# First two products with w1 of the first chunk, computed in halves of 256 rows

## The reference

```
x = x + tanh(g_xattn) * cross_attention(layernorm(x), ctx)     # 16 heads of 32, 154 keys a batch
h   = relu(layernorm(x) @ w1.T + b1)                           # 2048 hidden features
hq  = float_quantize(h, 4, 3)                                  # 8-bit float
out = float_quantize(hq @ float_quantize(w2, 4, 3).T + bq, 5, 10)
x = x + tanh(g_ffn) * out
```

## Time and profile before

| | us |
|---|---|
| median of 3 runs | 1613.96 (1610.55 to 1615.25) |
| the profiled execution | 1612.67 |
| its span, first to last instruction | 1610.9 |
| PE busy in the span | 1533.0 (95%) |
| PE idle in front of `hidden(0, 0)` | 7.2 |
| mean granted TensorE clock, share of full speed | 0.987 |

### The profile page before, as it was taken

How to read it: one execution, slowest core, us unless ns; L and a number is a source line. 1 busy time by engine, 2 the same in 40 slices (tenths; PEclk the granted TensorE clock), 3 DMA queues, 4 the chain that set the end, 5 groups by cost and what they waited for, 6 DMA issues and landing times.

```text
span 1610.9 us, 23580 instructions
## 1 busy us (share of the span) xinstructions
PE 1533.0 (95%) x8576; PEld 694.5 (43%) x8576; DVE 944.7 (59%) x1297; ACT 813.1 (50%) x1196; POOL 877.4 (54%) x919
## 2 busy tenths in 40 slices
PE   7875999999999999999999999999999999999998
PEld 4421444444444444444444444444444444444443
DVE  7787465675756566564656656465665656446231
ACT  4665664635545463555546455554645455454411
POOL 3788464554736455474646547464654746445320
PEclk9997999999999999999999999999999999999999
DMA  8356463544544454344435444344543434333120
GB/s 335 94 156 147 135 144 103 140 105 115 112 132 100 113 135 103 105 114 137 103 110 135 113 99 110 125 101 125 136 114 102 110 120 102 99 99 85 43 53 26
DMA packets 252856, 186.70 MB, mean 116 GB/s; under 512 B 160013, under 2 KB 209477, under 8 KB 251077
## 3 DMA queue, kind: packets, MB, share of 16 engines
q1 hardware_dynamic: 252740, 185.19, 42.9%
HBM read 99.95 MB, written 51.59 MB: 94 GB/s over the span
## 4 chain that ended last, share of the span: by engine, by line
PE 72%; DVE 13%; POOL 5%; issue 5%; DMA 1%; ACT 1%; SPq 1%; DVEq 0%; ACTq 0%
PE ring L514 52%; PE ring L708 8%; PE m_ps L616 4%; DVE y L1014 3%; PE s_ps L646 2%; DVE bns L1039 2%; DVE resid L1056 2%; PE y_ps L674 2%; DVE xn L1065 1%; PE d_ps L663 1%; POOL rs L1161 1%; POOL x L1149 1%; DVE smax L992 1%; PE s_ps L639 1%; DVE resid L1026 1%
## 5 line engine op out<-in xcount | busy, mean ns | idle before, releaser
L514 PE MATMUL ring<-late_a,w 128*128 128x512 f16 x3072 | 703.8, 380 | 7.2 <-issue 7.2
L514 PEld LDWEIGHTS ring<-late_a,w 128*128 128x128 f16 x3072 | 297.8, 98 | 355.0 <-issue 23.7
L815 ACT ACTIVATE late_b<-ring,b_sb,wsc 128x512 fp8e4<-128x512 f32 x256 | 199.3, 779 | 419.8 <-PE ring L514 419.8
L1123 POOL TENSOR_TENSOR pmain<-p,pmain 128x512 f16<-128x512 f32 x256 | 303.8, 1189 | 177.4 <-ACT p L793 175.8
L992 DVE TENSOR_REDUCE smax<-m_ps 128x4 f32<-128x616 f32 x256 | 203.4, 795 | 209.5 <-PE m_ps L616 209.2
L1014 DVE RECIPROCAL y<-d_ps 128x256 f32<-128x256 f32 x128 | 223.5, 1746 | 97.3 <-PE d_ps L666 95.1
L793 ACT ACTIVATE p<-s_ps,prob_log,sc 128x512 f32<-128x512 f32 x320 | 247.9, 775 | 0.9 <-POOL pleft L1123 0.9
L708 PE MATMUL ring<-w,late_b 128*128 128x512 fp8e4 x1024 | 229.7, 381 | 1.5 <-ACT late_b L815 0.9
L790 ACT ACTIVATE pmain<-s_ps,prob_log,sc 128x512 f16<-128x512 f32 x256 | 198.2, 774 | 5.9 <-PE s_ps L646 5.7
L1123 POOL TENSOR_TENSOR pleft<-p,pleft 128x512 f16<-128x512 f32 x64 | 76.6, 1197 | 213.0 <-ACT p L793 213.0
L514 PE MATMUL ring<-wo,yT 128*128 128x512 f16 x768 | 175.1, 381 | 0.0
(11 more groups left out here) (149 smaller groups left out, 1413.8 us busy)
## 6 DMA issues: line engine op xcount, KB each, us to landing
qstack<-q_rows SPq DMA_DIRECT2D x192, 128.0 KB, 3.0
pstack<-left_rows SPq DMA_DIRECT2D x192, 128.0 KB, 2.6
xin<-in_x SPq DMA_DIRECT2D x64, 256.0 KB, 3.3
q_rows<-qparts SPq DMA_DIRECT2D x32, 512.0 KB, 2.8
left_rows<-pleft SPq DMA_DIRECT2D x64, 256.0 KB, 2.5
resid<-in_x SPq DMA_DIRECT2D x64, 256.0 KB, 3.1
out_x<-resid SPq DMA_DIRECT2D x64, 256.0 KB, 2.3
resid<-in_w_t SPq DMA_DIRECT2D x5, 1024.0 KB, 6.2
```

The lines of the kernel that those rows point to most:

```text
L514: last = pe.matmul(dst, lhs(a, k), rhs(b, k), start=(k == 0 and p == 0), stop=(k == n_k - 1 and p == 2))
L815: nc.scalar.activation(hT[:, j, :], ring_bank("h", c, j)[:], ACT.Relu, bias=b1_sb[:, j:j + 1], scale=wsc[:, j // 4, 1:2], saturate=False). ...
L1123: nc.gpsimd.tensor_tensor(part[:, 1, :], p32[:, n % 2, :], part[:, 0, :], ALU.subtract).then_inc(prob_lo, 1)
```

## The change

`hidden(0, 0)` and `hidden(0, 1)` are each computed in two halves of 256 columns of `x2T` (256 rows of the chunk, two tiles). The first halves of both stand at beat 40 and wait only for the transposes of tiles 0 and 1. The second halves stand where the whole products stood: that of product 0 at beat 41, that of product 1 at beat 42 behind `value(1, 1)`. Each half is 12 matmuls of 128x256 into its half of the same bank; the semaphore that lets `relu` read the bank is raised by the second half. All other products, and all the other engines' programs, stay as they are.

```
+HIDDEN_HALVES = {0: 40, 1: 40, 2: 41, 3: 42}
...
+            def hidden_half(n):
+                half, j = divmod(n, 2)
+                if j == 0:
+                    for landed in x2t_in:
+                        pe.wait_ge(landed, (half + 1) * 2 * DMA)
+                if n == 0:
+                    pe.wait_ge(w1_ready, W1_ORDER.index(0) + 1)
+                if half == 0:
+                    ring_free("h", 0, j)
+                cols = slice(half * HALF_COLS, (half + 1) * HALF_COLS)
+                last = product(ring_bank("h", 0, j)[:, cols], lambda a, k: w1[:, 0, a, k, j * P:j * P + P],
+                               lambda b, k: x2T[:, b, k, cols], KT)
+                if half:
+                    last.then_inc(hid_done, 1)
...
-                run(hidden, HIDDEN_AT, beat)
+                once(hidden_half, HIDDEN_HALVES, beat)
+                run(lambda c, j: hidden(c, j) if c or j > 1 else None, HIDDEN_AT, beat)
```

## The result

The changed kernel takes 1607.51 us (median of 20 runs, 1605.19 to 1610.15), the kernel before 1612.33 us (20 runs, 1610.12 to 1615.25). The ratio is 0.9971, 95% interval 0.9965 to 0.9978: a gain of 4.8 us by the medians, just inside the 0.3% that counts as no change here, but clear of zero. A repetition gave 0.9977 (0.9966 to 0.9989), 3.6 us. One of the 12 executions of wait_all took 2023.27 us; without it the median is 1612.34 instead of 1612.35.

A forecast was written before the change was run, and what follows sets the result against it. PE, busy 95% of the span, bounds the kernel; early halves fill its 7.16 us idle time. From the median 1613.96, minus 2.6 us (half clock up to 165 us, shift wait included), it predicted 1611.4 us, range 1608.1 to 1614.5.

The forecast's parts named there:

- part 1: First halves at beat 40: 24 matmuls, 2.6 to 5.2 us, all in PE's idle time before 160.15, costing nothing.
- Rival B: Gain eaten by weight loads not hidden at 256 columns, or half clock to the end; 1613.4 to 1613.96, chance 0.12.
- (c): Half clock from 160.15 through all of the stretch: lift_main(1, 8) at 169.05, a gain of 0.6 us.
- Rival D: The change does nothing: first halves can't start before the later tiles have landed; chance 0.03.
- part 3: A new wait before lift_left(1, 2) for the shift's four DMAs, landing at 162.5; loses about 1 us of the gain.
- The sum, by clock: Start of lift_main(1, 8), before at 169.65, worked out for three courses of the clock; gains of 4.0, 2.6 or 0.6 us.
- (a): Everything from 160.15 at full clock: lift_main(1, 8) at 165.65, a gain of 4.0 us.
- (b): Half clock up to 165 us, then full: lift_main(1, 8) at 167.05, a gain of 2.6 us; the value taken.
- Rival A: Clock stays up (4.0 us) and no fall at 250 us (1.7 us): together 5.7 us, 1608.3; chance 0.13.
- Rival C: Slower: clock falls at the 13 later waits, about 1.7 us each, 22 us at all, 1633; chance 0.04.

The follow-up runs named there:

- wait_all: The changed kernel, but the first halves wait for the transposes of all four tiles; 1612.35 us, ratio 0.9999 to the kernel before.
- dve_order: The changed kernel with VectorE's softmax shift of chunk 1 put in front of the low part of w1's last quarter; 1605.63 us, ratio 0.9959 to before.
- after_fill_250: The changed kernel with 8 matmuls, their result overwritten, in front of the rank at beat 67; 1606.29 us, ratio 0.9967 to the kernel before.
- fill_250: The kernel before with 8 matmuls, their result overwritten, in front of the rank at beat 67; 1610.77 us, ratio 0.9994.
- fill_local: The changed kernel with the early half of product 1 computed twice into the same place; 1608.33 us, ratio 0.9974 to the kernel before.
- w2_later: The kernel before with ScalarE converting w2's last quarter one beat later, 57 instead of 56; 1612.24 us, ratio 0.9998.
- a_again: The changed kernel executed again, unchanged; 1608.57 us, ratio 0.9977 to the kernel before.
- a_look: The changed kernel, unchanged, a single execution for a profile; 1611.54 us.
- a_look3: The changed kernel, unchanged, a single execution for a further profile; 1608.60 us.
- both: The changed kernel with the order of dve_order and the repeated early half of fill_local; 1606.21 us, ratio 0.9962 to the kernel before.

## Why the prediction was wrong, point by point

**Right: where PE stood and why.** The 7.16 us were a wait for the last transpose; the second half starts 7.9 us behind the rank in every profile of the changed kernel, as the whole product did (160.15 - 152.32 = 7.83), and wait_all shows that without the early start there is no gain.

**Right: part 1.** The first halves lie wholly in the idle time (they end 5.8 us behind the rank at low clock, 4.5 where the clock comes up during them). The price of a half product at full clock was put at 1.3 us and is 1.32. 12 loads of 98 ns and 12 matmuls of 256 columns on the same 128 rows take 1.32 us together, so the loads are hidden, and Rival B's first branch is out. This contradicts the rule that the prediction took from the Trainium skill, "TensorE: Matmul & The Clock Gate", by which a weight load overlaps with running matmuls only on other row groups; the rule stands there in the section "The mechanism" and not in the one named. Rival B's second branch, half clock through all of it, comes near to the first profile (a gain of 1.0 us, against the 0.6 of (c)), but to no other. Rival D is out: the first halves start 0.46 us behind the start of the rank (151.58 - 151.12).

**Right: part 3.** lift_left waits 1.07 us for the shift's DMAs, and dve_order, whose stretch is shorter by as much as these DMAs and the transposes are earlier, bears out that they bound it.

**Wrong: the clock, in "The sum, by clock".** I worked out (a), full clock, as a gain of 4.0 us, and (b), half clock up to 165 us, as 2.6, and took (b), with the sentence "Our idle time is the longer one, so part of the stretch behind it will be slow". This step failed. In four of five profiles it is not slow. The two early halves bring the clock up by 156 to 158 us, and it stays up, through 3.41 to 3.44 us of idle time in three of them and 2.09 in the fourth; the stretch gains 17.24 - 13.59 = 3.65 us instead of 2.6. Case (a) was sized well: from the rank to lift_main it has 165.65 - 152.32 = 13.33 us, measured are 13.59. The 2.05 us wait, on which I built, is followed by a fall in one of four profiles of before and two of five after. I had read one execution of it as a threshold. The length of the idle time alone doesn't decide: 3.44 us passed without a fall, 2.86 us did not, and the same 2.09 us was followed by a fall in one execution and by none in another. The 2.6 us of (b) are not far from the average of 3.1, but by luck: that average is made of four stretches of 13.6 us and one of 16.29. Only after_fill_250 has the course of (b), slow first and then fast, and there the clock is back sooner and the stretch is 13.86 us instead of the 14.73 (167.05 - 152.32) of the sum.

**Not in the sum: the wait for w2's last quarter.** The prediction said that no other engine has a backlog and that everything behind moves along. That holds for the engines, but it took no account of a 1 MB load whose time varies: ScalarE waits for it 0.96 to 2.23 us in the four profiles of before, 0 to 0.86 in the five of the changed kernel, and the middle is shorter by 1.2 us in the mean. Whether the change causes it stays open. fill_250, which is the kernel before up to its filler at 249 us, has no such wait and a middle of 56.88 us, and fill_local, with the changed kernel's early halves, waits 1.08 us. In four of the changed kernel's five profiles the issue of the load takes 1.3 to 1.8 us and the transposes come later; in all four of before it takes 0.43. wait_all, whose halves don't start early, has the long issue too, but its time is that of before, and taking the wait away (w2_later) gave nothing that can be measured. So of the 4.8 us the runs explain the stretch's 3.1; the rest, 0.5 us by the repetition and 1.7 by the first result, is not shown to have a cause.

**Rival A** put the larger gain on a clock that stays up and on the missing fall at 250 us together. The first half of it is what happened; the second is not shown to be tied to the change. **Rival C**, falls at the later waits, did not come in any profile: the two matmuls of a rank behind such a wait take 0.42 us everywhere after 255 us.

**The base.** I counted from the median of three runs, 1613.96. Twenty runs have 1612.33. So of the 3.9 us between 1611.4 and 1607.51, 1.6 are the base and 2.2 the size of the gain. Even with (b) the forecast from the longer row would have been 1609.7, and 1607.51 lies only 0.6 us under the end of the range: the base decided that, as much as the clock.

## What to carry to other kernels

Work moved into an idle time in front of a critical stretch can pay twice: by its own length, and because TensorE can be at full clock when the stretch begins. In the one profile with one early half the clock stayed low until 163 us; with two it was up before 158 us in every profile. Look behind the moved wait for the next DMA in the same queue; here it took 1.1 us of the gain. Moving the VectorE instruction that held up both that DMA and the last transpose shortened the stretch by 1.3 us; the wait between the two stayed at 1.07 us.

Don't read a rule on the clock from one profile. Two more executions of the kernel before would have shown that the fall at 250 us comes and goes.

## What the runs showed of the hardware

TensorE stood for 3.41 to 3.44 us at 2.4 GHz, between two groups of matmuls, without losing the clock (a_again, a_look, a_look3). In other executions it lost it within 2.86 us of standing (after_fill_250), behind a wait of 2.05 us (3 of the 9 profiles in the table), and, in the first profile, while 12 matmuls ran behind 2.09 us of standing.

A POOL subtraction of 128x512 took 2.54 us when a VectorE instruction of 128x2048 had started 0.8 us before it, and 1.15 us without it. In dve_order another POOL instruction of 128x512 started just before VectorE's (156.22 against 156.23 us); there POOL's took 1.16 us and VectorE's 3.29 instead of 2.34.

The issue of one 1 MB load took 0.43 us in one profile of the changed kernel and 1.3 to 1.8 in four. Where it was long, in these and in wait_all, the load landed 6.1 to 6.6 us after its start; where it was short, 7.2 to 8.6 us in the same two kernels, but 6.3 us in fill_250, 6.7 in fill_local and 5.4 in the kernel called both.
